# Edge stages of a graph-attention layer: one-hots from spread 16-bit codes, four gather buffers in place of three

## What is computed

```python
e     = leaky_relu(alpha_s[src] + alpha_d[dst], 0.2)       # 4 heads
ex    = exp(e - segment_max(e, dst)[dst])
s     = segment_sum(ex, dst)
out   = segment_sum(h[src] * (ex / s[dst])[:, :, None], dst)
```

## Time and profile before

| | |
|---|---|
| median of 3 runs | 3336.28 us (3321.86 to 3338.29) |
| profiled execution | 3329.73 us |
| its span, first to last instruction | 3328.1 us |
| indirect DMAs of the edge stages | 1568, that is 196 chunks of 8 |
| mean granted TensorE clock | 0.82 of full speed |

### The profile page before, as it was taken

How to read it: one execution, slowest core, us unless ns; L and a number is a source line. 1 busy time by engine, 2 the same in 40 slices (tenths; PEclk the granted TensorE clock), 3 DMA queues, 4 the chain that set the end, 5 groups by cost and what they waited for, 6 DMA issues and landing times. The chain is left out here.

```text
span 3328.1 us, 53733 instructions
## 1 busy us (share of the span) xinstructions
PE 2231.7 (67%) x11831; PEld 1712.6 (51%) x11832; DVE 1730.3 (52%) x4175; ACT 1302.8 (39%) x2646; POOL 1946.3 (58%) x1918
## 2 busy tenths in 40 slices
PE   0726667677667667744665666666666755999996
PEld 0424455455445455433454544444544545999984
DVE  3645455555555555564554554454554556555545
ACT  0514344444444444431333433333433333444445
POOL 0256666666566666627666666666666631666654
PEclk9968788888888888877777777777777777999998
DMA  2623333333333333333344433333343325556545
GB/s 52 210 77 93 98 98 95 94 100 94 94 100 95 93 96 95 97 111 101 104 112 107 111 107 104 106 105 106 102 112 107 106 74 149 104 103 105 103 93 167
DMA packets 245595, 347.83 MB, mean 105 GB/s; under 512 B 87442, under 2 KB 184105, under 8 KB 245513
## 3 DMA queue, kind: packets, MB, share of 16 engines
q0 software_dynamic: 101728, 251.76, 30.5%
q1 hardware_dynamic: 103081, 52.72, 6.3%
q10 hardware_dynamic: 40720, 42.61, 3.8%
HBM read 292.90 MB, written 54.42 MB: 104 GB/s over the span
## 5 line engine op out<-in xcount | busy, mean ns | idle before, releaser
L912 POOL DMA_INDIRECT gathered<-table,idx x1568 | 1594.3, 1017 | 859.4 <-issue 452.5
L1204 PE MATMUL psA_e<-gathered,hotf 128*128 128x260 f32 x3136 | 873.6, 433 | 112.7 <-issue 87.3
L1204 PEld LDWEIGHTS psA_e<-gathered,hotf 128*128 128x128 f32 x3136 | 668.2, 219 | 259.5 <-issue 117.9
L1090 ACT ACTIVATE hotT<-psT 128x1024 bf16<-128x1024 bf16 x196 | 199.6, 1019 | 890.3 <-DMA x_in<-in_x 815.6
L968 DVE TENSOR_TENSOR gathered<-gathered,psDW_e 128x2048 f32<-128x2048 f32 x98 | 224.0, 2286 | 315.8 <-ACT psDW_e L1095 269.0
L968 DVE TENSOR_TENSOR gathered<-gathered,psW_e 128x2048 f32<-128x2048 f32 x98 | 223.9, 2285 | 244.8 <-ACT psW_e L1095 205.4
L1086 ACT ACTIVATE hotf<-hot 128x1024 f32<-128x1024 bf16 x196 | 206.1, 1052 | 273.7 <-remote 129.8
L1615 POOL DMA_INDIRECT moe_d<-xscaled,xtarget x113 | 179.3, 1587 | 124.6 <-DVE xtarget L1559 53.8
L948 DVE TENSOR_TENSOR hot<-iota,code_r 128x1024 bf16<-128x1024 bf16 x196 | 240.1, 1225 | 2.9 <-issue 2.9
L1587 PEld LDWEIGHTS xpsH<-xxT,w1e 128*128 128x128 f32 x1808 | 220.7, 193 | 6.2 <-ACT xxT L1516 0.4
L1596 PE MATMUL xpsO<-w,hidT 128*128 x904 | 217.1, 383 | 9.4 <-DVE hidT L1548 8.0
(11 more groups left out here) (309 smaller groups left out, 3415.9 us busy)
## 6 DMA issues: line engine op xcount, KB each, us to landing
gathered<-table,idx POOLq DMA_INDIRECT x1568
w<-in_L_ffn_w ACTq DMA_DIRECT2D x8, 2048.0 KB
xb<-in_L_ffn_b SPq DMA_DIRECT2D x113, 128.0 KB
w<-xnT_d SPq DMA_DIRECT2D x98, 128.0 KB
table<-acc POOLq DMA_DIRECT2D x49, 130.0 KB, 2.5
table<-acc ACTq DMA_DIRECT2D x49, 130.0 KB
xnT_d<-xnT ACTq DMA_DIRECT2D x49, 128.0 KB, 1.8
xf_d<-w ACTq DMA_DIRECT2D x49, 128.0 KB
```

What stands on the lines that cost most here:

```text
L912: pool.indirect_dma_start(out=G[:, q, k, :], out_offset=None, in_=table, in_offset=bass.IndirectOffsetOnAxis(ap=idx[:, q, k:k + 1], axis=0 ...
L1090: act.activation(hotT[:, q, :, :], psT[:], ACT.Copy).then_inc(s["hotT"], 1)
L1204: ins = pe.matmul(psA[:, par, 0:GW], hotf[:, q, k, :], G[:, q, k, :], start=(k == 0), stop=(k == KT - 1))
```

## The change

The source codes are also stored in DRAM as 16-bit numbers, one row of 1024 for each chunk, and SP loads that row spread over all 128 partitions. The one-hot with window places on partitions (`hotT`) is then one comparison with the partition's own number (`mark`). The turning on PE and both copies on ACT go; DVE makes the float32 one-hot `hotf` itself, in a new step `placed` between `edge_scale` and `gain`, and the bf16 `hot` is gone. `hotT`, `hotf`, `dwin` and `codes` have two buffers, `gathered` and `idx` four. The loop's body has four turns, the tile buffers two in place of three. On PE `add` comes second in the list. `psD` and `psW` have banks of their own in both stages. The wait of `targets` for `edge_scale` goes. The edge preparation gets eight more DVE instructions and one store.

```diff
-SLOTS = 3
+SLOTS = 4
+TURN = 2
@@ prepare_edges
+            sp.wait_ge(s["coded"], 1)
+            sp.dma_start(codes_d.rearrange("(c e) -> c e", e=CE), code_c[:]).then_inc(s["stored"], 16)
+            chain.link(dve.tensor_scalar(rel_c[:], low[:], ends[0:NC, 0:1], None, ALU.subtract))
+            dve.tensor_scalar(residue_c[:], by_chunk_i[:], P - 1, None, ALU.bitwise_and)
+            chain.link(dve.tensor_scalar(rel_c[:], rel_c[:], 7, None, ALU.arith_shift_right))
+            dve.wait_ge(s["tiled"], 1)
+            dve.tensor_copy(high[:], residue_c[:])
+            chain.link(dve.tensor_copy(low[:], rel_c[:]))
+            chain.link(dve.scalar_tensor_tensor(low[:], low[:], float(P), high[:], ALU.mult, ALU.add))
+            dve.tensor_scalar(code_c[:].rearrange("c (k p) -> c p k", k=KT), low[:].rearrange("c (p k) -> c p k", k=KT), float(1 << 14), None, ALU.min).then_inc(s["coded"], 1)
@@ gat_edges, SP
             def load(g, c, q, par, use):
-                sp.wait_ge(s["logits"], g + 1)
+                hold(sp, s["logits"], g + 1, s["tick"])
...
+            def load_codes(g, c, q, par, use):
+                hold(sp, s["hotT"], g + 1, s["tick"])
+                sp.dma_start(codes[:, par, :], codes_d[ds(c * CE, CE)].rearrange("(o e) -> o e", o=1).to_broadcast([P, CE])).then_inc(s[f"codes_in{par}"], 16)
...
-                rounds = chunks(sp, new_pass(sp), nothing, (0, load), (1, load_x, True))
+                rounds = chunks(sp, new_pass(sp), nothing, (0, load), (-1, load_codes), (1, load_x, True))
@@ gat_edges, DVE
             def one_hot(g, c, q, par, use):
-                dve.tensor_tensor(hot[:, q, :, :], iota[:].rearrange("p (k f) -> p k f", k=1).to_broadcast([P, KT, P]),
-                                  code_r[:, ds(c * KT, KT)].rearrange("p (k f) -> p k f", f=1).to_broadcast([P, KT, P]), ALU.is_equal).then_inc(s["hot"], 1)
+                dve.wait_ge(s[f"codes_in{par}"], g * 8 - par * 8 + 16)
+                dve.tensor_scalar(hotT[:, par, :, :].rearrange("p k f -> p (k f)"), codes[:, par, :], mark[:, 0:1], None, ALU.is_equal).then_inc(s["hotT"], 1)
...
+            def placed(g, c, q, par, use):
+                dve.wait_ge(s["added"], g + SLOTS - 1)
+                dve.tensor_tensor(hotf[:, par, :, :], iota[:].rearrange("p (k f) -> p k f", k=1).to_broadcast([P, KT, P]),
+                                  code_r[:, ds(c * KT, KT)].rearrange("p (k f) -> p k f", f=1).to_broadcast([P, KT, P]), ALU.is_equal).then_inc(s["hotf"], 1)
...
-                rounds = chunks(dve, both_new(dve), next_pass, (1, edge_logits), (-1, one_hot), (6, keys, True), (1, edge_scale), (3, gain), (5, denominators, True), (5, sums, True))
+                rounds = chunks(dve, both_new(dve), next_pass, (1, edge_logits), (-1, one_hot), (6, keys, True), (1, edge_scale), (0, placed), (3, gain), (5, denominators, True), (5, sums, True))
@@ gat_edges, ACT
-            def floats(g, c, q, par, use):
-                act.wait_ge(s["hot"], g + 1)
-                act.wait_ge(s["added"], g + 1)
-                act.activation(hotf[:, q, :, :], hot[:, q, :, :], ACT.Copy).then_inc(s["hotf"], 1)
-
-            def turned(g, c, q, par, use):
-                act.wait_ge(s["turned"], g + 1)
-                act.activation(hotT[:, q, :, :], psT[:], ACT.Copy).then_inc(s["hotT"], 1)
@@ gat_edges, PE
             def targets(g, c, q, par, use):
                 pe.wait_ge(s["dwin"], g + 1)
-                pe.wait_ge(s["hotT"], g + 2)
+                pe.wait_ge(s["hotT"], g + 3)
                 pe.wait_ge(s["target_read"], g + 1)
-                if attention and later(c, 1):
-                    pe.wait_ge(s["scaled"], g)
...
-            def turn(g, c, q, par, use):
-                pe.wait_ge(s["hot"], g + 1)
-                pe.wait_ge(s["hotT"], g + 1)
-                for k in range(KT):
-                    ins = pe.transpose(psT[:, k, :], hot[:, q, k, :], identb[:])
-                ins.then_inc(s["turned"], 1)
...
-                chunks(pe, nothing, nothing, (1, targets), (8, project, True), (0, turn), (7, fin_turn, True), (7, dots, True), (2, add), (3, values, True), (4, keys, True))
+                chunks(pe, nothing, nothing, (1, targets), (2, add), (8, project, True), (7, fin_turn, True), (7, dots, True), (3, values, True), (4, keys, True))
...
-                chunks(pe, nothing, nothing, (1, targets), (7, mix, True), (12, gates, True), (0, turn), (10, fin_turn, True), (2, add))
+                chunks(pe, nothing, nothing, (1, targets), (2, add), (7, mix, True), (12, gates, True), (10, fin_turn, True))
```

More of the change, by code:

```diff
@@ L203, in build @@
             windows = (code, code_r, lower, upper, first_tile, window_tile, passes)
-            edges = (identb, iota, acc, own, peak, parts, windows)
-            stage(prepare_edges, a, srcp, ident, identb, ones, iota, eps, code, lower, upper, first_tile, passes)
+            edges = (codes_d, partition, iota, acc, own, peak, parts, windows)
+            stage(prepare_edges, a, srcp, codes_d, partition, ident, identb, ones, iota, eps, code, lower, upper, first_tile, passes)
             spare = w1[:, 14:16].rearrange("p e k f -> p (e k f)")
@@ L223, in build, with prepare_edges @@
     nc.clear_and_free_semaphores([weights_in])
-def prepare_edges(nc, a, srcp, ident, identb, ones, iota, eps, code, lower, upper, first_tile, passes, sem):
+def prepare_edges(nc, a, srcp, codes_d, partition, ident, identb, ones, iota, eps, code, lower, upper, first_tile, passes, sem):
     with ExitStack() as ctx:
@@ L743, in _, with gat_edges @@
                 passes_over(pe, lambda r: None, step)
-def gat_edges(nc, layer, srcp, table, identb, iota, acc, own, peak, parts, windows, attention, last, sem):
+def gat_edges(nc, layer, srcp, table, codes_d, partition, iota, acc, own, peak, parts, windows, attention, last, sem):
     with ExitStack() as ctx:
@@ L851, in new_pass @@
         def new_pass(eng):
-            return lambda r: hold(eng, s["pass"], r * 2 + 2, s["tick"])
+            return lambda r: hold(eng, s["pass"], r * 3 + 3, s["tick"])
         def new_dest(eng):
@@ L896, in load_x @@
                     sp.dma_start(xnT[b], xnT_d[ds(i, 1), :, :].rearrange("o p f -> (o p) f")).then_inc(s[f"x_in{b}"], 16)
-                rounds = chunks(sp, new_pass(sp), nothing, (0, load), (6, load_x, True))
+                rounds = chunks(sp, new_pass(sp), nothing, (0, load), (-1, load_codes), (6, load_x, True))
             hold(sp, s["stored"], rounds * (PER_STORE * NT) + PER_STORE, s["tick"])
@@ L931, in _ @@
             dve.sem_inc(s["acc"], 4)
+            dve.sem_inc(s["hotT"], 2)
+            dve.tensor_copy(mark[:], partition[:]).then_inc(s["pass"], 1)
             dve.tensor_copy(code_r[:], code[:]).then_inc(s["pass"], 1)
@@ L1141, in _ @@
                 act.wait_ge(s["constants"], 32)
-                chunks(act, new_dest(act), nothing, (9, store, True), (6, roots, True), (0, floats), (0, turned), (1, exps), (6, divide, True), (5, squares, True), (7, relu, True), (8, copies, True))
+                chunks(act, new_dest(act), nothing, (9, store, True), (6, roots, True), (1, exps), (6, divide, True), (5, squares, True), (7, relu, True), (8, copies, True))
             else:
@@ L1172, in _ @@
                 act.sem_inc(s["gate_logits"], 1)
[L1173 removed]
+                chunks(act, new_dest(act), nothing, (9, store, True), (8, root, True), (1, exps), (13, gates, True), (11, xf_turned, True), (6, divide, True), (8, normalise, True))
                 act.wait_ge(s["gap"], 1)
```

84 lines of the change are left out of this document (43 added, 41 removed).

## The result

The changed kernel takes 3532.86 us (median; 3521.99 to 3536.72), the kernel before in the same runs 3334.06: a ratio of 1.0588, 95% interval 1.0558 to 1.0619. The forecast was 3108 us, the range 3000 to 3340. The profiled execution has a span of 3533.2 us at a mean granted clock of 0.797 (before 0.820).

The account below looks back on a forecast made before the run. POOL's gathers were taken as the floor, with PE's late signals keeping the edge stages above it. 3329.7 - 315 (floor reached) + 6.6 (preparation) = 3021 us; 87 us of long stalls left in made 3108; range 3000 to 3340.

Parts of the forecast that it names:

- What bounds the kernel: Edge stages: POOL's gathers are the floor at 10.53 us a chunk; 1.9 us of waits come from PE's late sums.
- The loop through ACT: ACT's copies and PE's turning go; exp waits for its own logits alone; delays of some 7 to 9 us are hidden.
- the wait moves: Rival: DVE waits at placed and its reduce as ACT did at hotT; 12.4 us a chunk, 3336 us; chance 0.07.
- SP and DMA: SP's queue: the added load of 51 MB over both stages costs nothing, with more than 5 us to spare behind load_x.
- The fourth buffer: POOL's gathers: one more period of slack, over 10 us against waits of at most 7.6 us, so usual waits go.
- DVE: DVE in the edge stages: the new 16-bit compare takes 0.70 us, costing nothing while POOL's 10.8 us cover it.
- Contention: POOL's gathers beside DVE's compares: the new compare adds 0.3 us a chunk, making the floor 10.8 us.
- Preparation: Edge preparation: eight more DVE instructions add 6.6 us, with ends of 5 and 10.
- Signals held until the gathers drain: Rival, edge stages: PE's signals wait out runs of four gathers; 13.8 us a chunk, 3603 us; slower, chance 0.18.
- PE becomes the bound: Rival: PE's clock stays low, stage 0 gains nothing, stage 1 reaches 10.9 us; 3194 us; chance 0.15 with other part-way limits.
- The floor is reached: Rival: both edge stages run at POOL's floor of 10.8 us a chunk; 3021 us, between 2990 and 3060; chance 0.27.
- What would show it: Signs in the new profile: gathers 10.5 to 10.9 us apart, added waits under 120 us, placed waits seldom over 3 us.

Follow-up runs that it names:

- e11: e4 with POOL waiting after the eight gathers of every second chunk until they have landed; 3350.38 us, ratio 1.0067.
- e10: e4 with POOL waiting after the eight gathers of every chunk until they have landed; 3563.98 us, ratio 1.0702.
- e6: e4 with a gather waiting for the add of the chunk three before in place of four, so the fourth buffer does nothing; 3314.84 us, ratio 0.9952.
- e1: The changed kernel with the load of idx one turn earlier in SP's list, ahead of the tile load; 3352.69 us, ratio 1.0055.
- e13: The changed kernel with a gather waiting for the add three chunks before in place of four, so the fourth buffer does nothing; 3314.96 us, ratio 1.0078.
- e16: e4 with SP issuing the spread load of the codes twice, the second into a buffer nothing reads; 3306.65 us, ratio 1.0061.
- e4: The changed kernel with idx loaded one turn earlier on SP and placed at offset 1 in DVE's lists; 3347.95 us, ratio 1.0025.
- run 185: Not a run label: in the changed kernel, 185 of 188 PE signals finished behind the eighth gather of a run of gathers are over 1 us late.
- e14: e4 with two psD buffers in stage 1 alone, where PE issues targets a chunk ahead; 3282.80 us, ratio 0.9978.
- e7: e4 with each indirect gather replaced by a plain DMA of 128 fixed neighbouring rows, issued by POOL; 2568.68 us, a single execution.
- e8: e4 with the gathers replaced by plain loads of fixed rows, issued by SP in place of POOL; 2571.51 us, a single execution.
- e12: e4 with each indirect gather taking its row numbers from one constant tile (rows 0 to 127); 3345.63 us, a single execution.

## Why the prediction was wrong, point by point

**What bounds the kernel** was half right. POOL does stop for `added`, and the 10.53 us of its own are there. But I took these stops for a slack that a buffer can fill. They are the same 2.4 to 3.7 us behind one or two chunks with three, four and six buffers. A forced wait for the landing behind every second chunk takes their place one for one (e11, 404 us of pauses against 411); behind every chunk it costs more (e10, 642).

**The loop through ACT** went as described, but was worth little: exp starts 0.04 us behind its logits (in the stretch above they end at 818.27, exp starts at 818.31), and 816 us of ACT's waits at `hotT` are gone, yet at best 0.5% of the time (e6). The waits moved to DVE, where the sum had allowed 87 us for the long ones: `both_e` from 257 us in 48 waits to 534 in 64, `hotf` 247 in 34. The rival "the wait moves" named this place, with a chance of 0.07.

**SP and DMA, "I cost it at nothing … I see more than 5 us to spare"**, is the step that failed first. I had counted `load_x` against the transfer of its own tile, not against `idx` of a later chunk behind it, and not together with the fourth buffer two paragraphs above, which lets POOL ask for that `idx` a turn sooner. What it cost is 363 us of POOL's waits for `idx`, where I had 0. Its price is 5.3% by e1 and 5.1% by e13, about 175 us. The added traffic itself costs at most 0.8% (e16).

**The fourth buffer, "over 10 us, against waits of at most 7.6 us … The usual waits go"**, is the second, and it is why no gain stands against the loss: at best it is worth nothing, by e6 against e4 it costs 0.7%. With the first step mended (e1) the kernel stands at 1.0055, not at the forecast's 0.93. The slack is in time, but a longer run of gathers makes the signals later: behind the eighth gather of a run 185 of 188 are late. The long ones come when POOL has stopped. As I read it, what decides is how many chunks' signals one stop lets through. `targets` of the next chunk cannot be issued before DVE has read the single `psD`, so it is one or two, and POOL's runs stay mostly at one or two chunks. e14 shows this limit move a little when `psD` is doubled; that it explains the rest of the 12.3 us is not shown.

**DVE.** The compare of 16-bit codes takes 0.486 us (median), not the 0.70 taken, inside the ends. The Trainium skill ("VectorE: DVE Perf Modes", "Mode 4×_2P — both tricks at once") gives an estimate of some 0.43 by its figures; the trace agrees within 0.06. The time does not hang on it.

**Contention** had the wrong sign: a gather takes 0.988 us in the mean where it took 1.017, so 0.23 us a chunk less in place of 0.3 more. The new compare costs next to nothing: the 165 gathers that run beside it alone take 0.946 us in the median like the others, and 2.9 us more in all. The 258 beside `placed` take 54 us more, the 348 beside the compare of before took 99. So the prediction's reading, that the new compare pays like the old, is not borne out here.

**Preparation**: 6.6 expected, 7.0 measured.

**The rivals.** "Signals held until the gathers drain" was the right mechanism with the wrong size. I let runs grow to four chunks and set its threshold at a pause of 6.5 us behind four; 52 of stage 1's runs are of one or two chunks, with 3.0 and 3.6 us behind them, so stage 1 takes 12.57, not 13.8. I had the rows for it: 33 long waits that ended with a run. I held against it that most signals come inside a run, which did not help: as I read it, the chain of one chunk needs two of them. "PE becomes the bound" did not come: PE is busy for 168 of 300 us in stage 0 and 169 in stage 1, at a granted clock of 0.78 and 0.76. "The floor is reached" did not either: without the loss of stage 0 a chunk still takes 12.2 to 12.4 us (e4, e6).

**What would show it**: the chunks of a run are 10.62 us apart (first gathers at 791.96 and 802.58), as said, and the compare (0.486 us) and the exp (at most 0.83 us behind the logits) are as said too. POOL's waits on `added` at 227 us (limit 120) and waits before `placed` of up to 16.5 us (seldom over 3) said wrong at once. Nothing in my list looked at `idx`.

## What to carry to other kernels

Whoever adds a buffer so that an engine may run ahead should list everything that this engine consumes, and look on each in-order queue at what stands in front of it: the buffer moves the need for `idx`, not only that for `gathered`. And a wait that ends with another engine's pause is not a slack that buffering fills; test it by forcing the pause (e11) before building on it. Of this change the parts without the fourth buffer are worth 0.5%, and only with `idx` loaded earlier and `placed` later (e6); without these two moves they lose 0.8% (e13).

## What the runs showed of the hardware

PE's signals reach DVE, ACT and SP late while POOL issues indirect gathers back to back. In the kernel before 372 of 634 are over 1 us late in the first eight gathers of a run and 82 of 84 behind them, up to 20.1 us. The longest come when POOL stops: all 85 waits over 11 us end in a pause of POOL. Of all late ones 113 of 479 come during a run. With plain loads of the same size, by POOL (e7) or by SP (e8), no signal is over 1 us late; with indirect gathers of fixed rows 241 of 380 and 195 of 197 are (e12). So it is the indirect form, not the bytes, plain loads as such or the rows' places. With the landing awaited for each chunk (e10) 21 of 244 are late, though gathers are in flight there too. The Trainium skill ("Perfetto Trace Analysis", "Per-engine timelines") says that a matmul's end in a trace is an estimate and that the signal is pushed once PSUM has acknowledged the writes; the increments are stamped late at the semaphores, but whether the acknowledgement or the way from there is held up, no run here tells. It also stays open whether the landing itself or POOL's standing still releases the long ones, for both fell together in every run, and why the first eight gathers of a run hold signals in e4 and e11 and hardly any in e10.
